# Recommendation tower: groups of three features, transposes two groups ahead, a ring of six gathered groups, two embedding buffers, pair products in portions

## What is computed

```python
e = jnp.stack([tbl_0[ids[:, 0]], ..., tbl_26[ids[:, 26]]], axis=1)      # (2048, 27, 128)
interactions = jnp.einsum('bfd,bgd->bfg', e, e)
z = jnp.concatenate([e.reshape(B, -1), interactions[:, _TRIU_I, _TRIU_J]], axis=1)
h = jnp.concatenate([z, dense_ctx], axis=1)                             # (2048, 3823)
h = jnp.maximum(h @ W_top1 + b_top1, 0.0)                               # 512 wide
h = jnp.maximum(h @ W_top2 + b_top2, 0.0)                               # 256 wide
y = h @ W_top3
```

## Time and profile before

| | |
|---|---|
| median of 3 runs | 590.26 us (589.81 to 592.77) |
| the profiled execution, its span | 769.5 us |
| instructions in the span | 15280 |
| TensorE matmul busy | 537.4 us (70%) |
| GpSimd busy (descriptors of gathers) | 415.9 us (54%) |
| ScalarE busy | 246.5 us (32%) |
| VectorE busy | 154.0 us (20%) |
| granted TensorE clock, mean | 0.856 |

### The profile page before, as it was taken

One profiled execution on the slowest core, in us unless ns is written; L12 is line 12 of the kernel. 1 busy time (PEld: TensorE's weight loads), 2 busy tenths in 40 slices (PEclk: granted clock), 3 DMA queues, 4 the chain that ended last, 5 costly groups with the idle time before them and its releaser, 6 DMA issues.

```text
span 769.5 us, 15280 instructions
## 1 busy us (share of the span) xinstructions
PE 537.4 (70%) x6224; PEld 434.5 (56%) x6224; DVE 154.0 (20%) x269; ACT 246.5 (32%) x370; POOL 415.9 (54%) x441
## 2 busy tenths in 40 slices
PE   3406856767578677876776787658778767677884
PEld 2304645656456555755555675546667555566773
DVE  3304211112021111211111221211111121121222
ACT  3414422233132233323233332332323233232441
POOL 6766463663646546564664656466465646556110
PEclk9858777999879798889899898987889898988997
DMA  6515311412414123241422424131332424133110
GB/s 208 172 49 179 96 45 43 73 49 67 51 61 56 47 72 42 75 52 35 84 49 75 45 78 51 59 58 47 76 45 77 52 67 47 48 77 46 56 41 7
DMA packets 52704, 51.10 MB, mean 66 GB/s; under 512 B 36652, under 2 KB 39897, under 8 KB 52680
## 3 DMA queue, kind: packets, MB, share of 16 engines
q0 software_dynamic: 13984, 28.42, 20.4%
q1 hardware_dynamic: 38696, 22.34, 9.9%
HBM read 40.22 MB, written 10.49 MB: 66 GB/s over the span
## 4 chain that ended last, share of the span: by engine, by line
PE 47%; another core or an unknown queue 20%; issue 19%; ACT 7%; DVE 2%; DMA 2%; SPq 1%; ACTq 0%; DVEq 0%
PE p_hid L572 12%; PE p_hid L573 11%; PE p_hid L574 11%; PE p_prod L637 7%; ACT emb L341 5%; PE p_quad L567 5%; DVE emb_low L446 2%; ACT emb_high L338 1%; PE p_hid_t L603 1%; DMA w_stage<-w_dense_dram 1%; ACT w_high L330 1%; SPq L226 0%; DMA pairs_dram<-prod 0%; DMA inter<-pairs_dram 0%
## 5 line engine op out<-in xcount | busy, mean ns | idle before, releaser
L301 POOL DMA_INDIRECT gathered<-tbl_dram,idx x432 | 412.5, 955 | 301.9 <-issue 125.0
L572 PE MATMUL p_hid<-w_high,emb_high 128*128 128x512 f32 x432 | 204.5, 473 | 156.1 <-DVE emb_low L446 95.4
L572 PEld LDWEIGHTS p_hid<-w_high,emb_high 128*128 128x128 f32 x432 | 95.5, 221 | 182.9 <-DVE emb_low L446 100.5
L573 PE MATMUL p_hid<-w_low,emb_high 128*128 128x512 f32 x432 | 190.6, 441 | 0.0
L338 ACT ACTIVATE emb_high<-p_quad 128x512 fp32r<-128x512 f32 (+1 forms) x111 | 66.3, 597 | 386.9 <-remote 183.6
L574 PE MATMUL p_hid<-w_high,emb_low 128*128 128x512 f32 x432 | 190.2, 440 | 0.0
L446 DVE TENSOR_TENSOR emb_low<-p_quad,emb_high 128x512 fp32r<-128x512 f32 (+1 forms) x112 | 75.2, 671 | 431.9 <-ACT emb L341 230.9
L341 ACT ACTIVATE emb<-p_quad 128x512 f32<-128x512 f32 (+1 forms) x111 | 128.9, 1161 | 0.0
L574 PEld LDWEIGHTS p_hid<-w_high,emb_low 128*128 128x128 f32 x432 | 94.4, 218 | 23.7
L573 PEld LDWEIGHTS p_hid<-w_low,emb_high 128*128 128x128 f32 x432 | 95.8, 222 | 18.0
L637 PE MATMUL p_prod<-emb 128*27 128x27 f32 x4096 | 53.6, 203 | 47.6 <-issue 47.0
(11 more groups left out here) (40 smaller groups left out, 237.6 us busy)
## 6 DMA issues: line engine op xcount, KB each, us to landing
w_stage<-w_dense_dram SPq DMA_DIRECT2D x27, 256.0 KB
gathered<-tbl_dram,idx POOLq DMA_INDIRECT x432
pairs_dram<-prod SPq DMA_DIRECT2D x16, 432.0 KB
pairs_dram<-prod SPq DMA_DIRECT2D x16, 208.0 KB
inter<-pairs_dram SPq DMA_DIRECT2D x187, 14.6 KB
w_stage<-w_dram SPq DMA_DIRECT2D x2, 256.0 KB
idx<-ids_dram SPq DMA_DIRECT2D x16, 13.5 KB
w_stage<-w_pairs_dram SPq DMA_DIRECT2D x1, 256.0 KB
```

The lines of the kernel that those rows point to most:

```text
L301: pool.indirect_dma_start(gathered[:, f, :], None, tables[f], bass.IndirectOffsetOnAxis(ap=idx[:, par, f:f + 1], axis=0),).then_inc(quad_g ...
L572: nc.tensor.matmul(dst, high, w_high, start=start, stop=False)
L573: nc.tensor.matmul(dst, high, w_low, start=False, stop=False)
```

## The change

Five things change together.

1. A group is 3 features instead of 4, so that there are 9 equal groups a tile.
2. The transposes run two groups ahead of layer 1, across the tile's border too.
3. `gathered` is a ring of 6 groups (18 features) that runs on over the tiles, in place of 27 places. The gather of a group waits for the transposes of the group six before it.
4. There are two `emb` buffers, and the 256 pair-product matmuls of a tile are cut into 8 calls of 32: calls 0 to 2 at the end of the tile, 3 to 5 after the next tile's first layer 1 group, 6 and 7 after its second. `layer2` moves two tiles behind, and the copies of products and the hidden layer on ScalarE and VectorE are set in new places.
5. The ids of tiles 1 to 15 come in one DMA, the weights have six staging slots, and GpSimd, SyncE, ScalarE and VectorE are written out without loops. `emb_high` and `emb_low` hold three groups instead of a whole tile. TensorE starts when the identity has landed and does not wait for the biases.

```diff
-    QUADS = [list(range(f, min(f + 4, NF))) for f in range(0, NF, 4)]
+    FEATS = 3
+    GROUPS = NF // FEATS
+    RING = 6
+    SPLIT = 3
-    STAGES = 4
+    STAGES = 6
+    CALLS = 8
...
-        gathered = sb("gathered", [P, NF, D])
-        emb = sb("emb", [P, P, NF])
+        gathered = sb("gathered", [P, RING, FEATS, D])
+        emb = [sb(f"emb_{k}", [P, P, NF]) for k in range(2)]
...
-            def gathers(t, par, loads):
-                wait(pool, ids_loaded[par], loads * 16, quads_free)
-                for q, quad in enumerate(QUADS):
-                    wait(pool, quad_transposed, (t - 1) * NQ + q + 1, quads_free)
-                    for f in quad:
+            pool.wait_ge(ids_loaded[0], 16)
+            for t in range(TILES):
+                if t == 1:
+                    pool.wait_ge(ids_loaded[1], 16)
+                for g in range(GROUPS):
+                    slot = ring_slot(t, g)
+                    wait(pool, group_transposed, t * GROUPS + g - RING + 1)
+                    for k in range(FEATS):
...
-            def tile(t, par, first=False):
-                other = (par + 1) % 2
-                if first:
-                    layer1_quad(t, 0, par, first)
-                for q in range(1, NQ):
-                    transpose_quad(t, q, par)
-                    if q > 1 or not first:
-                        layer1_quad(t, q - 1, par, first)
-                    if q == 5 and not first:
-                        layer1_pairs(t - 1, other)
-                if not first:
-                    transpose_hid1(t - 1)
-                pair_products(t, first)
-                transpose_quad(t + 1, 0, other)
-                layer1_quad(t, NQ - 1, par, first)
-                if not first:
-                    layer2(t - 1)
+            def tile(t, par, depth=2):
+                other = (par + 1) % 2
+                for g in range(GROUPS):
+                    if g < GROUPS - 2:
+                        transpose_group(t, g + 2, par)
+                    else:
+                        transpose_group(t + 1, g + 2 - GROUPS, other)
+                    layer1_group(t, g, par, depth == 0)
+                    if g == 0 and depth >= 1:
+                        pair_products(t - 1, other, [3, 4, 5])
+                    if g == 1 and depth >= 1:
+                        pair_products(t - 1, other, [6, 7])
+                    if g == 2 and depth >= 2:
+                        layer2(t - 2)
+                    if g == GROUPS - 2 and depth >= 1:
+                        layer1_pairs(t - 1, other)
+                    if g == GROUPS - 1:
+                        pair_products(t, par, [0, 1, 2])
+                        if depth >= 1:
+                            transpose_hid1(t - 1)
...
             def last_tile(t, par):
...
-                features(3, [3])
-                features(4, [0, 1])
-                transpose_quad(t, 6, par)
-                features(4, [2])
-                pair_products(t, False)
-                layer1_pairs(t - 1, (par + 1) % 2)
+                    if g == GROUPS - 3:
+                        transpose_group(t, GROUPS - 1, par)
+                pair_products(t, par, range(CALLS))
+                layer1_pairs(t - 1, other)
+                layer1_group(t, GROUPS - 1, par)
```

More of the change, by code:

```diff
@@ new lines, in copy_whole, with group_copies @@
+            def copy_whole(t, g):
+                if g == 0:
+                    wait(act, prod_bank_done, (t - 1) * NB)
+                f0 = g * FEATS
+                nc.scalar.activation(emb[t % 2][:, :, f0:f0 + FEATS].rearrange("p b f -> p f b"),
+                                     bank_of(t, g), ACT.Copy).then_inc(group_copied, 1)
+            def group_copies(t, g):
+                if t == 0:
+                    for n in range(FEATS * g, FEATS * (g + 1)):
+                        weight_high(n)
+                act.wait_ge(group_transposed, t * GROUPS + g + 1)
+                if t == LAST and g == GROUPS - 1:
+                    copy_whole(t, g)
+                    copy_high(t, g)
+                else:
+                    copy_high(t, g)
+                    copy_whole(t, g)
+                if t == 0 and g == GROUPS - 1:
+                    for n in range(NF, len(STAGED)):
+                        weight_high(n)
@@ L540, in _ @@
             dve.wait_ge(zeroed, 1)
-            dve.wait_ge(consts_loaded, CONSTS * 16)
-            tile(0, 0, first=True)
-            tile(1, 1, second=True)
-            for t in range(2, 5):
-                tile(t, t % 2)
-            with dve.Fori(0, TILES // 2 - 3) as i:
-                for k in range(2):
-                    tile(2 * i + 5 + k, (1 + k) % 2)
-            tile(TILES - 1, (TILES - 1) % 2, final=True)
-            last = TILES - 1
-            last_inter_to_low(last, [0])
@@ new lines, in last_tile @@
+            def last_tile(t, par):
+                other = (par + 1) % 2
+                for g in range(GROUPS - 1):
+                    if g < GROUPS - 3:
+                        transpose_group(t, g + 2, par)
+                    layer1_group(t, g, par)
+                    if g == 0:
+                        pair_products(t - 1, other, [3, 4, 5])
+                    if g == 1:
+                        pair_products(t - 1, other, [6, 7])
+                    if g == 2:
+                        layer2(t - 2)
+                    if g == GROUPS - 3:
[3 more added lines that the diff above has]
+                layer1_group(t, GROUPS - 1, par)
```

399 lines of the change are left out of this document (181 added, 218 removed).

## The result

| | before | after |
|---|---|---|
| median, same call | 590.54 us (589.81 to 592.77, 4 runs) | 645.53 us (637.06 to 647.08, 4 runs) |
| ratio, 95% interval | | 1.0851 [1.0779, 1.0924] |
| profiled execution: time, span | ahead of the prediction | 644.36 us, 642.4 us |

The forecast was 591.2 us, with a range of 572 to 600. The medians differ by 55 us, and the time is outside the range. The ratio counts the two faster of the four runs after (644.36 and 637.06 us) alone, and by it the change costs 50 us.

What follows compares the result with a forecast made beforehand. GpSimd's gathers were taken as the bound: 2.8 + 542.1 + 1.5 + 32.5 = 578.9 us, with 11.4 us left outside the span. The change added only 0.9 us at the tail: 590.3 + 0.9 = 591.2 us, range 572 to 600.

Steps and rivals of the forecast that it cites:

- what bounds the kernel before: Timed kernel as a whole: GpSimd's 432 gathers bind, 33.8 us a tile against TensorE's 30.9.
- 2.8 + 542.1: GpSimd's chain: first gather at 2.80 us, then 432 gathers with their plain gaps, 542.1 us.
- Setting the waits of the first profile aside: Profile of before: durations and spacings were used, its waits not, since its span was 769.5 us against 590.26 timed.
- the late news: TensorE's finished transposes reach ScalarE and GpSimd about 6 us late in the profile; set aside for the timed runs.
- the return of GpSimd's loop: GpSimd's loop in the kernel before: its return costs nothing that shows, bounded by 4.6 us; taken as 0.
- gathers, ids, ring at the start: GpSimd: gathers and ring cost 0, first gather stays at 2.8 us, the large load of ids is hidden.
- Rival B: Tile 1, slower: the ring stops GpSimd if weights are done later than 66 us; 600 us at 75; chance 0.12.
- All of it lies under the gathers (33.8 against 30.9 us a tile): 0: TensorE's moved portions, two `emb` buffers, earlier transposes and later `layer2`: same matmuls at other places, cost 0.
- Loops written out ... I take 0: Loops of the engines: removing the returns was judged by GpSimd's gaps at its return, 4.97 against 4.94 us; 0.
- rival C: GpSimd's 7 loop returns, faster: a fetch stop at each goes away; at 1 us each 584 us; chance 0.04.
- The median leaves 11.4 us for what lies outside the span: Launch and end: 11.4 us between the gathers' sum of 578.9 us and the timed median.
- The tail's +0.9 us: End of last tile: nine layer 1 matmuls, 2.07 us, before the pair products, less a former 1.2 us wait.

Runs made afterwards that it cites:

- before_third: The kernel before, unchanged, run and profiled once more at the lower level: 589.75 us.
- two_portions: Kernel after with pair products in two portions instead of three and copies one group earlier, all work and TensorE's loop kept: 593.48 us, 1.0018 of before.
- peel: Kernel after with tile 2 taken out of TensorE's loop, which then begins at tile 3: 601.04 us, 1.0146 of before.
- W: Not a run but a theory of the experiments: the pair products come too late at TensorE, which waits for them (`inter_low`).
- one_chunk_2: Kernel after with 4 of the 12 loads of pair products a tile, part of layer 1 using old data, lower level: 591.98 us, 1.0045 of before.
- pad128: Kernel after with 128 added identity transposes (256 instructions) at TensorE's start, upper level: 1.0338 of before.
- pad64: Kernel after with 64 added identity transposes (128 instructions) at TensorE's start, upper level: 0.9877 of before.
- pad192: Kernel after with 192 added identity transposes (384 instructions) at TensorE's start, upper level: 1.0022 of before.
- before_shift: Kernel before with TensorE's loop begun one tile earlier, at tile 2: 591.38 us, 0.9974 of before.
- pe_unrolled_2: Kernel after with TensorE's loop over tiles 2 to 13 written out, lower level: 600.88 us, 1.0125 of before.
- pe_unrolled: Kernel after with TensorE's loop over tiles 2 to 13 written out, upper level: 0.9868 of before.

## Why the prediction was wrong

**Right: what bounds the kernel before.** The chain of before_third, 54% GpSimd, no gather gap over 0.4 us, the last gather's end at 546.7 where the sum had 2.8 + 542.1 = 544.9. Setting the waits of the first profile aside was right too, but my reason was only half so: the late news is not the profiler's, and timed runs at the upper level have it.

**Right in size, misread: the return of GpSimd's loop.** The gather of the earlier trace rows at 542.82 is not the first after the return. The trace has GpSimd's branch at 535.21, and the first gather behind it has no more than a plain gap:

```profile
535.66 0.94 POOL L301 DMA_INDIRECT gathered<-tbl_dram,idx  x1 [0.31 <-DMA idx<-ids_dram]
```

So the term of 0 was better founded than its bound of 4.6 us said.

**Right: gathers, ids, ring at the start.** Rival B had the ring stopping GpSimd in tile 1. The first gather is at 2.70 in the kernel after. The weights were split at 54.5 us in before_third (I had 59) and at 49.4 in the kernel after, and there GpSimd does not stop before 236 us. Its 51.6 us of waits begin behind the first long return. Two_portions, with the same ring, has none beyond plain gaps.

**Wrong, the failed step: "All of it lies under the gathers (33.8 against 30.9 us a tile): 0".** The cover was 2.9 us a tile and the sum of TensorE's work did fit. What I had not done is to follow the pair products' round trip at its new place. With the last portions behind the next tile's second group, the way starts 16.1 us of TensorE's work before it is wanted. The way takes 19.4, and 9.4 of it is SyncE issuing 12 loads, as many as in before_third. That is 3.25 us a tile and more than the cover: 30.9 + 3.25 = 34.2, where GpSimd needs 33.8. Over 14 tiles this makes an estimated 5 us; measured, TensorE ends 9.3 us further behind the last gather in peel than in before_third (15.9 against 6.6). Taking 8 of the 12 loads away made the wait 6.4 us in all. Alone W is worth 1.2% to 1.5%, 7 to 9 us: with it in the sum I would have said 598 to 600, at the edge of my range. The wait itself is the lesser part of the miss; it used up the cover under which the next term lay.

**Wrong: "Loops written out ... I take 0".** I looked at the returns of GpSimd, which the change takes out, and not at the one loop that it keeps, TensorE's. The price of its return went from 0.2 us to 4.3-4.8, with another 2.0 behind it and a stretch at the lower clock: 9.6 us each, four times. That return was nearly under the gathers as long as W was not there (one_chunk_2, 1.0045). With W it is on the path, and is worth 43 us. That the long return would come was not to be read from the kernel before, whose own TensorE loop returns in 0.21 to 0.25 us.

The Trainium skill, "Runtime: NRT & Kernel Launch", § Instruction fetch mechanics, says that instructions are fetched in blocks of 16 KiB, 256 of them, and that a taken branch to one that is no longer held stops the engine. I had it as rival C and on the wrong engine. The trace agrees in this: with each long return of the kernel after nine packets of 16384 bytes come on the instruction queue (the first two in the one of 390 us at 390.64 and 391.22), with its one short return none, in the loop of the kernel before none, and 55 - 19 packets between pad128 and pad64 are four times nine. A period of 256 instructions fits long, short, long, short at 0, 128, 256 and 384 as well. The trace differs where the page says that only two blocks are held: by that every return of a body of 1594 instructions would fetch, and the short ones come without a packet. The page also gives TensorE room for 2048 instructions, which would be eight blocks; a body of 1594 touches seven or eight of them, by where it starts. From the places of the first branch in the traces (after 2793, pad64 2921, pad128 3050, pad192 3175, peel 3583, two_portions 2857, the kernel before 3895, before_shift 3106, counted in recorded instructions) one can lay the blocks so that the long ones are those with eight. That is argued from the counts. No run here shows where the blocks lie or why eight should be too many, and the single short returns among long ones stay unexplained.

**Off in size: the tail.** "The median leaves 11.4 us for what lies outside the span": it is 2 us. The missing 9.1 are in three terms of the sum: the last gather lands 6.6 us after its end and not 1.5 (5.1), from the last transposes to the end it is 34.7 us and not 32.5 (2.2), and the last gather ends 1.8 later. The sum came to 590 by a fitted term, which is why it looked closed. The middle of what the Trainium skill, "Runtime: NRT & Kernel Launch", § The ~15µs preamble/postamble breakdown, gives for launch and end, 12 us, fitted the gap and was no evidence.

**The tail's +0.9 us** can't be told apart. The kernels with short returns or none, and W gone or lessened, are at 589.28 to 594.62 us, 1.0002 to 1.004 of before.

**What stays open.** The kernel after was not measured at the upper level and the padded ones not at the lower. Why pad192 is 1.5% above pad64 with equally short returns was not tried; 128 more transposes at the start are in it. No version of the changed kernel beats the kernel before at the lower level. The best with all work in it is two_portions, 1.0018.

## What to carry to other kernels

When a step is moved, follow what it produces all the way to who wants it, with every DMA issue on the way as time of the issuing queue: here 12 loads at 0.78 us were half of the trip, and the trip was longer than the cover by 3 us. Two delays that each nearly hide under the same bound do not hide together: add up the slack that is used, per tile, before putting down a zero. And if a kernel keeps one loop of some 1600 instructions on an engine, look at its branch times and the instruction queue after any edit, since moving it by 128 instructions changed the time by 24 to 36 us here, at the upper level.

## What the runs showed of the hardware

- TensorE's loop return takes 0.21 to 0.26 us or 4.3 to 5.1 us, and the place of the same loop decides whether long ones occur. The long one goes with nine packets on the instruction queue. It is followed by 2.0 us more without work ahead of the first layer 1 matmul, and by matmuls 0.43 us apart in place of 0.23.
- Straight-line code may not be free of it either. Without a loop, the pair products of the tail stop for 4.71 us behind nothing that the profile names, here in pe_unrolled_2. A packet of the instruction queue lies in that stop (569.94 to 573.37 us); that it is the cause is not shown. The kernel before stops for 2.11 us at the same place (before_third).

```profile
568.14 2.19 PE L590 MATMUL p_prod<-emb 128*27 128x27 f32 x227
575.04 0.41 PE L590 MATMUL p_prod<-emb 128*27 128x27 f32 x29 [4.71 <-issue]
```

- All kernels of a set are at one of two levels, 590 or 770 us for the kernel before. At the upper one ScalarE and GpSimd see TensorE's transposes late by several us, some 20 to 30 times. The order of the kernels differs there: pe_unrolled and pad64, the changed kernel without long returns, are 1.2% to 1.6% faster than before, while pe_unrolled_2 is 1.25% slower at the lower level.
- The landing of a gather took 1.7 us at the start and 6.6 us at the end of before_third, with the same 128 rows.
